# DVE's order in the odd steps of a causal long convolution: product before the gather

## The reference

```python
# L0_attn: STAGES = 3, causal, T = 2048, D = 256
xp = (X @ Wp + bp).reshape(B, T, 4, D)
f = (sine_positional_encoding(T, D) @ Wf + bf).reshape(T, 3, D)
xp, f = padded with T zeros in time
y = xp[:, :, 0, :]
for i in range(3):
    conv = irfft(rfft(y, axis=1) * rfft(f)[None, :, i, :], n=2 * T, axis=1)
    y = conv * xp[:, :, i + 1, :]
x = layernorm(X + y[:, :T])
# L0_ffn: HIDDEN = 768, int weights scaled by 1/127
x = layernorm(x + (silu(x @ wg.T) * (x @ wu.T)) @ wd.T)
```

## Time and profile before

| | |
|---|---|
| median of three runs | 760.33 us |
| the profiled execution, its own time | 762.3 us |
| its span, first to last instruction | 760.5 us |
| mean granted PE clock | 0.995 of full speed |
| PE busy | 730.5 us (96%) |
| DVE busy | 554.1 us (73%) |
| ACT busy | 488.0 us (64%) |
| POOL busy | 421.8 us (55%) |

### The profile page before, as it was taken

The page is one execution under the profiler, slowest core; times in us unless marked ns, Lnnn a source line. Parts: engine busy times, 40 slices in busy tenths (PEclk is TensorE's granted clock), DMA queues, the critical chain, the costliest instruction groups (busy, mean ns, idle before and its releaser), DMA issues.

```text
span 760.5 us, 16073 instructions
## 1 busy us (share of the span) xinstructions
PE 730.5 (96%) x5936; PEld 547.8 (72%) x5936; DVE 554.1 (73%) x1083; ACT 488.0 (64%) x962; POOL 421.8 (55%) x483
## 2 busy tenths in 40 slices
PE   6999999999899999999999999789999999999995
PEld 5878878888788888888888888545665556655663
DVE  4797778777688888888888888665656666565644
ACT  3445553444378888788887665446776776777753
POOL 3445554445243444344434444789788878888653
PEclk9999999999999999999999999999999999999998
DMA  8659768999898999989999996622445335452412
GB/s 290 212 179 333 248 213 282 316 320 305 297 259 256 260 259 246 257 254 263 254 248 265 310 258 218 225 56 56 103 93 114 109 84 112 85 137 57 63 54 79
DMA packets 193676, 152.69 MB, mean 201 GB/s; under 512 B 35776, under 2 KB 177216, under 8 KB 193344
## 3 DMA queue, kind: packets, MB, share of 16 engines
q1 hardware_dynamic: 191744, 146.36, 66.5%
q10 hardware_dynamic: 1856, 5.31, 2.2%
HBM read 109.45 MB, written 34.34 MB: 189 GB/s over the span
## 4 chain that ended last, share of the span: by engine, by line
PE 86%; DVE 5%; DMA 4%; issue 2%; ACT 2%; POOL 1%; SPq 0%; DVEq 0%; POOLq 0%; ACTq 0%
PE bank L472 21%; PE bank L398 20%; PE bank L452 18%; PE bank L493 10%; PE bank L411 7%; PE bank L432 3%; PE bank L433 3%; PE bank L434 3%; DMA toep<-filter_rows 1%; DVE prod L830 1%; DMA wi<-in_WDT 1%; DMA gates<-toep 1%; DMA xt<-in_XT 1%; DVE yl L864 1%; PE bank L509 1%
## 5 line engine op out<-in xcount | busy, mean ns | idle before, releaser
L1025 POOL TENSOR_TENSOR y<-y,gate 128x512 f32<-128x512 f32 (+1 forms) x108 | 124.7, 1160 | 172.3 <-DVE y L855 160.1
L398 PE MATMUL bank<-wps,xs 128*128 128x512 f32 x768 | 183.3, 398 | 7.9 <-DVE wps L788 6.5
L452 PE MATMUL bank<-prod,ei 128*128 128x256 f32 x720 | 186.8, 382 | 0.0
L398 PEld LDWEIGHTS bank<-wps,xs 128*128 128x128 f32 x768 | 144.7, 190 | 40.5 <-POOL xs L1052 8.1
L830 DVE TENSOR_TENSOR prod<-bank,wfx 128x512 f32<-128x512 f32 x180 | 124.2, 690 | 43.5 <-PE bank L411 43.5
L1052 POOL TENSOR_TENSOR xs<-xt,xs 128x256 fp32r<-128x256 f32 x128 | 93.7, 743 | 101.4 <-ACT xs L605 101.3
L472 PE MATMUL bank<-xh,wq 128*128 128x512 f16 x384 | 145.6, 379 | 0.2
L472 PE MATMUL bank<-xl,wq 128*128 128x512 f16 x384 | 145.5, 379 | 0.0
L1044 POOL TENSOR_TENSOR hl<-hf,hh 128x512 f16<-128x512 f32 x95 | 110.7, 1168 | 53.0 <-ACT hh L669 53.0
L452 PEld LDWEIGHTS bank<-prod,ei 128*128 128x128 f32 x720 | 123.4, 191 | 11.6
L634 ACT ACTIVATE y<-bank,iscl 128x512 f32<-128x512 f32 x96 | 66.0, 687 | 90.3 <-PE bank L434 90.3
(11 more groups left out here) (81 smaller groups left out, 1220.0 us busy)
## 6 DMA issues: line engine op xcount, KB each, us to landing
toep<-filter_rows SPq DMA_DIRECT2D x43, 1024.0 KB, 7.6
gate<-gates SPq DMA_DIRECT2D x48, 512.0 KB, 4.1
xt<-in_XT SPq DMA_DIRECT2D x31, 512.0 KB, 5.5
gates<-st SPq DMA_DIRECT2D x24, 512.0 KB, 4.1
gates<-toep SPq DMA_DIRECT2D x24, 512.0 KB, 4.2
xr<-in_X SPq DMA_DIRECT2D x16, 512.0 KB, 4.6
out_x<-oo SPq DMA_DIRECT2D x15, 512.0 KB, 3.2
toep<-filter_rows SPq DMA_DIRECT2D x10, 512.0 KB, 6.3
```

What stands on the lines that cost most here:

```text
L398: mm = pe.matmul(b_proj[n % PBK][:, :], xs[:, n % XSS, hx, k, :], wps[:, hw, k, p * 512:(p + 1) * 512], start=(k == 0 and q == 0), stop=(k ...
L452: mm = pe.matmul(b_out[m % 2][:, half * W:(half + 1) * W], ei[:, h, e0 * P:(e0 + 1) * P], prod[:, n % 3, h, :], start=(h == 0), stop=(h == 1))
L1025: nc.gpsimd.tensor_tensor(y[:, u % NG, a:a + count, :], y[:, u % NG, a:a + count, :], gate[:, a:a + count, :], ALU.mult).then_inc(gated, 1)
```

## The change

In DVE's odd steps k = 5, 7, ..., 13 of every unit, the product of the step now comes before the gather. In step 15, which has no product, nothing changes. In unit 11 the statistics of step 5 still stand behind both. No instruction is added or taken away, and no wait is changed.

```diff
                         if k <= 1 and u >= 1:
                             gather(u - 1, NPAIR - 2 + k)
-                        if k >= 5 and k % 2 and u < NU:
-                            gather(u, (k - 5) // 2)
                         if k % 2 == 0 and u + 1 < NU:
                             low(u + 1, k // 2)
                         if u < NU and k < NE:
                             multiply(u, k)
+                        if k >= 5 and k % 2 and u < NU:
+                            gather(u, (k - 5) // 2)
```

## The result

The changed kernel takes 769.88 us (median of 4, 768.22 to 770.41), before 760.33 us (median of 4, 760.05 to 763.13): a ratio of 1.0121, 95% interval 1.0106 to 1.0136, so slower by 8.1 to 10.3 us. The forecast was 767.8 us, within 763.2 to 771.5. The profiled execution took 770.41 us, with a span of 768.6 us against 760.5; the mean granted clock was 0.994 of full speed, and 0.995 before.

What follows compares the result with a forecast made beforehand. The prediction took PE to bound the kernel, at 86% of the span. The loop's 8.3 us less 0.8 in unit 11 gave +7.5 on the median 760.33, so 767.8 us, with 8 in 10 between 763.2 and 771.5.

Steps and rivals of the forecast that it cites:

- What bounds the kernel: PE takes 86% of the span; in the loop the gather's old place ahead of the odd product costs nothing.
- The odd product: In DVE's odd steps it starts 0.53 us after PE's state, as before: gain 0.
- The gather and its readout: In the loop the later gather makes PE's waiting readout 0.15 us late per pair of steps, 55 pairs: 8.3 us.
- rival C: Faster: the loop absorbs the gather, only unit 11 counts, 759.0 us; decides from a gather 0.07 us shorter on; chance 0.02.
- The even product: In the loop its delay would make PE's state 0.03 us late, hidden behind the readout's 0.15 us.
- The overlap of DVE's operations: In the loop DVE's next operation starts 0.61 us after a 0.69 us product; without overlap a pair costs 0.23 us.
- rival B: DVE becomes the loop's bound if its operations lose their overlap or ACT's input is late: 772.2 us, chance 0.14.
- The last unit: In unit 11 the first feed-forward matmul comes 0.87 us early, POOL and ACT up to 0.6 late; taken as -0.8 us.
- Sum: Loop and unit 11 together: 8.3 - 0.8 = +7.5 us on the profiled execution, 762.3 to 769.8 us.

Runs made afterwards that it cites:

- bank3_after: The changed kernel with a third PSUM bank for the readouts in units 0 to 10: 763.67 us, ratio 1.0037 to the kernel before.
- gather_last: The changed kernel with the gather moved further back, behind the low half in steps 6 to 14: 803.79 us, ratio 1.0566 to before.
- short_gather: The changed kernel with the gathers of steps 5 to 13 in units 0 to 10 on 224 of 256 columns: 766.21 us, ratio 1.0059 to before.
- last_root: The kernel before with, in the last unit, products first in steps 11 and 13 and POOL's second root ahead of step 11's gate: 759.73 us, ratio 0.9980.

## Why the prediction was right, point by point

*What bounds the kernel.* Right for the loop: the old place of the gather was free, and PE is the chain there in both kernels. At the border to the feed-forward part of the changed kernel it is POOL.

*The odd product.* Right: product 5 still starts 466.01 - 465.48 = 0.53 us after its state.

*The gather and its readout.* Right in mechanism and nearly in size. The forecast took 0.07 for signal and start and 0.08 for the exposed load, 0.15 a pair; measured are 0.158 by the units' marks, with a readout of 0.97 and not 0.95. The loop makes 8.7 us and not 8.3. That the wait is the cause is shown from both sides: with room for one more pair (bank3_after) it goes, and with the gather 0.60 later (gather_last) it grows by 0.60 a pair. That more than half of it, 0.09, is the weight load is shown by short_gather. The statement in rival C that a gather 0.07 shorter would free the loop was wrong, as it put the limit at the matmul's start; the limit lies at the weight load's start, 0.11 earlier. The prediction weighed what the Trainium skill (TensorE: Matmul & The Clock Gate, Architectural detail: the array is 16× 32×32, not 1× 128×128) says of weight loads that go ahead of matmuls in flight. The traces agree where nothing waits, with a readout's load 0.11 us ahead of its matmul (465.70 and 465.81); behind a late gather both start at 467.41, so no load passed its wait.

*The even product.* Right: hidden, with its own 0.03 a pair seen as 0.035 once the readout's wait was gone.

*The overlap of DVE's operations.* Right: 0.61 and 0.65 us from start to start, as before, so rival B's lost overlap did not occur. The even product comes 1.86 us after the odd one, as foreseen.

*The last unit.* This term was wrong. The forecast was -0.8 us and the net is about -0.1. PE's part was right (0.87 foreseen, 0.90 measured), and so was the late gate and root on POOL. What failed is the overlap: the prediction had POOL's work late beside PE's first feed-forward block, and took PE's rows alone, as if that cost nothing. It pushed POOL's gates beside L895 instead, both became slower, POOL's own work became the chain, and PE's block behind it was stretched by 0.76. An estimate from the rows of how much the slowing counts: with the two gates at 1.96 and not 2.94 us the sixth L903 would come 24.18 - 0.98 = 23.20 us after the transposes by POOL's chain, ahead of the 23.41 that last_root shows. By that estimate the late gate alone would have cost nothing.

*Sum.* The profile gives 8.7 - 0.1 = 8.6 us against 7.5 forecast, and 8.1 to 10.3 measured. The two errors, 0.4 in the loop and 0.7 in the last unit, go the same way, so nothing was balanced by luck; the median's difference is 9.55, and the 0.9 above the profile's sum lies within the interval and is not explained. The two profiled executions differ by 8.1 in span. In them other things vary that the change does not touch: the loop starts 0.8 us earlier in the one of after (product 0 at 200.76 and 201.59), and once in each a filter's DMA holds a unit up, by about 0.5 and 1.1 us.

## What to carry to other kernels

An instruction that releases another engine has two prices to read before it is moved: how long the one it makes room for now waits, and when the one it releases is next needed. Here the odd product had 0.20 us of idle time ahead of it, so it could gain nothing, while the gather's new place left it no slack towards the readout that waits for its bank. A PE wait costs from the moment at which the weight load would have been issued, not from the matmul's start, so slack has to be measured to the load. And a gain on the chain at the border of two stages can be lost, as here, when the same edit makes the engine late that feeds the next stage: follow that engine's work up to where the chain needs it.

## What the hardware showed that was not expected

A DVE operation with two SBUF inputs and POOL's products with all operands in SBUF slow each other: L895 takes 1.23 us in the median of its 15, 1.53 with POOL's gates beside its start, and 2.15 with them beside nearly all of it, while the two gates go from 1.96 to 2.94 us. In each case where a POOL operation runs as L895 starts, L895 ends 1.08 us after that operation's end, however long it lay beside it: 505.22 and 506.30 before, 513.20 and 514.28 in the changed kernel, 502.54 and 503.62 in last_root. The narrow gate that starts beside it in the changed kernel in turn ends only 0.58 us after L895. So the one waits for nearly all of the other. The Trainium skill (SBUF — State Buffer, SBUF: two separate sides) states that such a DVE operation and a GpSimd operation that reads SBUF take one pair of ports in turn; the trace agrees with these numbers, and the prediction should have weighed this at the last unit. The gather, the product and the low half, each with one input in PSUM, keep 0.74 to 0.75, 0.69 and 0.68 us beside POOL's gates.
